# Two-layer graph network on one core: the neighbour mean split in f16 and turned by a DMA transpose instead of by TensorE

## The reference

```python
# layer 0
mask = (adj > 0)
agg  = mask @ x / max(sum(mask, 1), 1)            # the neighbour mean
out0 = relu(concat(x @ W_self + b_self, agg @ W_nb + b_nb) @ W_comb + b_comb)
x1   = layernorm(x + out0)
# layer 1
ws   = leaky_relu(attention(x1) @ attention(neigh).T)
ws   = softmax(where(adj > 0, ws, -9e15))
out  = layernorm(x1 + concat(x1 @ Wfx + bfx, ws @ (neigh @ Wv + bv)))
```

## Time and profile before

| what | value |
|---|---|
| time, median of 3 runs | 728.27 us (727.76 to 729.59) |
| time of the profiled execution | 729.11 us, its span 727.3 us |
| busy share of the span | PE 93%, VectorE 86%, ScalarE 79%, GpSimd 18% |
| DMA | 141.40 MB, mean 194 GB/s |
| matmul and transposing instructions on PE | 7368 |

### The profile page before, as it was taken

How to read it: one execution, slowest core, us unless ns; L and a number is a source line. 1 busy time by engine, 2 the same in 40 slices (tenths; PEclk the granted TensorE clock), 3 DMA queues, 4 the chain that set the end, 5 groups by cost and what they waited for, 6 DMA issues and landing times.

```text
span 727.3 us, 19837 instructions
## 1 busy us (share of the span) xinstructions
PE 677.6 (93%) x7368; PEld 599.3 (82%) x7368; DVE 622.4 (86%) x1537; ACT 571.3 (79%) x928; POOL 130.7 (18%) x243
## 2 busy tenths in 40 slices
PE   5779889999999999999999999999999999997775
PEld 4668767888888888988888888888888888886554
DVE  5888578999989999999999999999999999987863
ACT  2555248888888888888888888888888888889893
POOL 0010121212222211222211112222111222212101
PEclk9999999999999999999999999999999999999997
DMA  8977999999999999999999999999999999731222
GB/s 258 370 168 163 251 286 239 195 213 213 195 220 197 194 226 204 200 219 211 221 219 203 212 223 194 215 218 191 219 206 205 210 206 214 165 75 37 38 37 44
DMA packets 260312, 141.40 MB, mean 194 GB/s; under 512 B 225528, under 2 KB 243832, under 8 KB 260216
## 3 DMA queue, kind: packets, MB, share of 16 engines
q1 hardware_dynamic: 259688, 140.10, 90.3%
q10 hardware_dynamic: 528, 0.03, 0.0%
HBM read 81.37 MB, written 4.19 MB: 118 GB/s over the span
## 4 chain that ended last, share of the span: by engine, by line
PE 78%; DVE 5%; ACT 5%; issue 4%; DMA 3%; SPq 3%; POOL 1%; POOLq 0%; ACTq 0%; DVEq 0%
PE ps_v L1174 21%; PE agg_both L1129 14%; PE agg_both L1132 14%; PE ps_t L1153 10%; PE s_both L1144 7%; PE agg_both L1193 3%; PE agg_both L1196 3%; DMA neigh_sb<-neigh_sb 2%; PE s_both L1033 1%; PE ps_x L1213 1%; PE ps_x L1216 1%; ACT score L936 1%; DMA neigh_sb<-in_L_gnn_neigh_dram 1%; SPq L405 1%; PE agg_both L1184 1%
## 5 line engine op out<-in xcount | busy, mean ns | idle before, releaser
L1129 PE MATMUL agg_both<-x,mask_t 128*128 128x257 f16 x1024 | 244.0, 274 | 3.1 <-DMA mask_t<-mask 3.1
L1132 PE MATMUL agg_both<-x,mask_t 128*128 128x256 f16 x1024 | 237.9, 274 | 1.6 <-DVE x L546 1.6
L930 ACT ACTIVATE score<-s_both,sc 128x512 f32<-128x512 f32 x256 | 178.4, 697 | 63.9 <-PE s_both L1144 58.2
L707 DVE CUSTOM_DVE_ANT_0 score<-score,mask 128x512 f32<-128x512 f32 x256 | 176.0, 687 | 16.8 <-ACT score L930 14.3
L1174 PEld LDWEIGHTS ps_v<-v,late 128*128 128x128 f16 x2304 | 144.0, 97 | 41.2 <-DVE late L771 16.6
L1174 PE MATMUL ps_v<-v,late 128*128 128x129 f16 (+1 forms) x2304 | 162.7, 219 | 11.3 <-DVE late L788 5.7
L936 ACT ACTIVATE score<-score,exp_bias,sc 128x1024 f32<-128x1024 f32 x128 | 159.2, 1244 | 3.2 <-DVE exp_bias L716 3.2
L771 DVE TENSOR_TENSOR late<-ps_t,late 128x512 f16<-128x512 f32 x192 | 130.8, 681 | 33.1 <-ACT late L943 31.3
L943 ACT CAST late<-ps_t 128x512 f16<-128x512 f32 x192 | 114.4, 596 | 20.5 <-PE ps_t L1153 20.5
L1153 PE MATMUL ps_t<-ident,score 128*128 128x128 f32 x768 | 116.8, 275 | 4.0 <-ACT score L936 3.7
L1129 PEld LDWEIGHTS agg_both<-x,mask_t 128*128 128x128 fp8e4 x1024 | 100.6, 98 | 17.3 <-DMA mask_t<-mask 3.3
(11 more groups left out here) (140 smaller groups left out, 801.0 us busy)
## 6 DMA issues: line engine op xcount, KB each, us to landing
adj_sb<-in_adj_dram SPq DMA_DIRECT2D x128, 512.0 KB, 5.3
neigh_sb<-in_L_gnn_neigh_dram SPq DMA_DIRECT2D x8, 512.0 KB, 7.9
score<-in_x_dram SPq DMA_DIRECT2D x8, 512.0 KB, 8.6
x_in<-in_x_dram SPq DMA_DIRECT2D x32, 128.0 KB, 3.0
out_dram<-out_sb SPq DMA_DIRECT2D x32, 128.0 KB, 3.5
mask_t<-mask SPq DMA_TRANSPOSE x128, 4.7
neigh_sb<-neigh_sb SPq DMA_TRANSPOSE x64, 4.0
mask<-in_L_gnn_W_comb_dram SPq DMA_DIRECT2D x1, 512.0 KB, 8.0
```

Of the source, the lines that this page charges most:

```text
L707: dve.tensor_tensor_reduce(score[:, b % 2, part], score[:, b % 2, part], mask[:, b % MASK_BUFS, part], 1.0, -3.0e38, ALU.subtract, ALU.max ...
L930: act.activation(score[:, b % 2, k * GW:(k + 1) * GW], ps_s[k % 2][:, :], ACT.Prelu, alpha=SLOPE, scale=score_scale).then_inc(leaky_made, 1)
L1129: mm = pe.matmul(agg[:, 0:D + 1], mask_t8[:, c, 0, :], x16[:, c, X_HI:X_ONE + 1], start=(c == 0), stop=(c == NC - 1), skip_group_check=True)
L1132: mm = pe.matmul(agg[:, 0:D], mask_t8[:, c, 0, :], x16[:, c, X_LO:X_LO + D], start=False, stop=False, skip_group_check=True)
```

## The change

The mean is scaled and split into two f16 halves straight from `ps_agg`, before it is turned: `mean_high` (ScalarE, slot 8) and `mean_low` (VectorE, slot 9). One DMA transpose, `turn_mean` (SP, slot 10), turns both halves (128 x 512 f16) into `mean_t`. PE's two transposes, the ScalarE activation of `mean_of` and their semaphores go. `combine` and everything behind it stand one slot further on, and so do the four mask quarters; `aggregate`, `degrees` and `turn_x` keep their slots.

```diff
-MASK_SLOTS = (-7, -5, -1, 0)
+MASK_SLOTS = (-6, -4, 0, 1)
 MEAN_AT = 8
-MEAN_T_AT = 9
-MEAN_SPLIT_AT = 10
-MEAN_LOW_AT = 11
+MEAN_LOW_AT = 9
+MEAN_T_AT = 10
 X_TURN_AT = 4
-COMBINE_AT = 12
-LAYER0_AT = 13
+COMBINE_AT = 13
+LAYER0_AT = 14
...
-        mean = sb("mean", [P, D], F32)
-        mean_t = sb("mean_t", [P, 2, D], F16)
+        mean = sb("mean", [P, 2, D], F16)
+        mean_t = sb("mean_t", [P, 2 * DC, P], F16)
...
+            def turn_mean(b):
+                sp.wait_ge(mean_lo_made, b + 1)
+                at_least(sp, combined, b)
+                sp.dma_start_transpose(mean_t[:, :, :], mean[:, :, :].rearrange("p a d -> p (a d)")).then_inc(mean_t_in, 16)
...
                 if d := due(s, X_TURN_AT, 0):
                     turn_x(d[0])
+                if d := due(s, MEAN_T_AT, 0):
+                    turn_mean(d[0])
...
-            def mean_of(b):
+            def mean_high(b):
                 act.wait_ge(degree_step, 2 * (b + 1))
-                at_least(act, mean_t_done, b)
-                act.activation(mean[:, :], ps_agg[b % 2][:, 0:D], ACT.Copy, scale=row[:, 5:6]).then_inc(mean_made, 1)
-
-            def mean_high(b):
-                act.wait_ge(mean_t_done, b + 1)
-                at_least(act, combined, b)
-                act.activation(mean_t[:, 0, :], ps_agg[b % 2][:, 0:D], ACT.Copy, scale=x_scale).then_inc(mean_hi_made, 1)
+                at_least(act, mean_t_in, 16 * b)
+                act.activation(mean[:, 0, :], ps_agg[b % 2][:, 0:D], ACT.Copy, scale=row[:, 5:6]).then_inc(mean_hi_made, 1)
...
-            def mean_transpose(b):
-                pe.wait_ge(mean_made, b + 1)
-                for dc in range(DC):
-                    mm = pe.transpose(ps_agg[b % 2][:, dc * P:(dc + 1) * P], mean[:, dc * P:(dc + 1) * P], ident[:, :])
-                mm.then_inc(mean_t_done, 1)
-
             def combine(b):
                 if b == 0:
                     pe.wait_ge(m_split, DC)
                 pe.wait_ge(x_t_in[b % 2], 16 * (b // 2 + 1))
-                pe.wait_ge(mean_lo_made, b + 1)
+                pe.wait_ge(mean_t_in, 16 * (b + 1))
```

More of the change, by code:

```diff
@@ L51 @@
 RES_BUFS = 4
-MASK_SLOTS = (-7, -5, -1, 0)
+MASK_SLOTS = (-6, -4, 0, 1)
 MEAN_AT = 8
-MEAN_T_AT = 9
-MEAN_SPLIT_AT = 10
-MEAN_LOW_AT = 11
+MEAN_LOW_AT = 9
+MEAN_T_AT = 10
 X_TURN_AT = 4
-COMBINE_AT = 12
-LAYER0_AT = 13
[L63 to L74, removed]
+COMBINE_AT = 13
+LAYER0_AT = 14
+X1_AT = 16
+X1_T_AT = 17
+X1_COPY_AT = 18
+X1_LOW_AT = 19
+HIDDEN_AT = 20
+TANH_AT = 21
+XATT_AT = 22
+STACK_AT = 23
+SCORE_AT = 24
+ROW_MAX_AT = 32
+TURN_AT = 34
+WEIGH_AT = 35
 BY_DMA = 1
@@ L82 @@
 EXP_PLACE = [[quarter for _, quarter in EXPS].index(k) for k in range(4)]
[L83 to L87, removed]
+WIDE_HIGH_AT = (36,)
+WIDE_LOW_AT = (37,)
+WIDE_TURN_AT = (38,)
+WIDE_WEIGH_AT = (41,)
+LAYER1_AT = 43
 SLOTS = NG * (NB - 1) + LAYER1_AT + 1
@@ L294, in gnn_kernel @@
         pv_done = sem("pv_done")
-        mean_t_done = sem("mean_t_done")
+        mean_t_in = sem("mean_t_in")
         combined = sem("combined")
@@ L312, in gnn_kernel @@
         exp_made = sem("exp_made")
-        mean_made = sem("mean_made")
         mean_hi_made = sem("mean_hi_made")
@@ L720, in degrees @@
                 dve.wait_ge(agg_done, NQ * (b + 1))
-                at_least(dve, mean_made, b)
-                dve.tensor_scalar(row[:, 4:5], ps_agg[b % 2][:, D:D + 1], EDGE_F8, x_scale, ALU.max,
-                                  ALU.mult).then_inc(degree_step, 1)
+                at_least(dve, mean_hi_made, b)
+                dve.tensor_scalar(row[:, 4:5], ps_agg[b % 2][:, D:D + 1], EDGE_F8, None, ALU.max).then_inc(degree_step, 1)
                 dve.wait_ge(degree_step, 2 * b + 1)
@@ L728, in mean_low @@
                 dve.wait_ge(mean_hi_made, b + 1)
-                dve.scalar_tensor_tensor(out=mean_t[:, 1, :], in0=ps_agg[b % 2][:, 0:D], scalar=x_scale,
-                                         in1=mean_t[:, 0, :], op0=ALU.mult, op1=ALU.subtract).then_inc(mean_lo_made, 1)
+                dve.scalar_tensor_tensor(out=mean[:, 1, :], in0=ps_agg[b % 2][:, 0:D], scalar=row[:, 5:6],
+                                         in1=mean[:, 0, :], op0=ALU.mult, op1=ALU.subtract).then_inc(mean_lo_made, 1)
             def layer0(b):
@@ L983, in _ @@
                 first_part(s)
-                if d := due(s, MEAN_SPLIT_AT, 0):
-                    mean_high(d[0])
                 if d := due(s, X1_AT, 0):
@@ L1004, in _ @@
                 if d := due(s, MEAN_AT, 0):
-                    mean_of(d[0])
+                    mean_high(d[0])
                 if d := due(s, LAYER1_AT + 1, 0):
@@ L1195, in combine @@
                 for k, ((r, w), dc) in enumerate(product(HI_LO, range(DC))):
-                    mm = pe.matmul(ps_agg[b % 2][:, 0:D], mean_t[:, r, dc * P:(dc + 1) * P], m16[:, w, dc, 0:D],
+                    mm = pe.matmul(ps_agg[b % 2][:, 0:D], mean_t[:, r * DC + dc, :], m16[:, w, dc, 0:D],
                                    start=False, stop=(k == 3 * DC - 1))
@@ L1229, in _ @@
                     aggregate(*d)
-                if d := due(s, MEAN_T_AT, 0):
-                    mean_transpose(d[0])
                 if d := due(s, COMBINE_AT, 0):
```

## The result

The changed kernel takes 840.53 us (median of 6 runs, 837.66 to 844.74), the kernel before 729.42 us in the same session (727.76 to 730.16): a ratio of 1.154, 95% interval 1.151 to 1.156. It is slower, as forecast, but by 111 us instead of 74, and outside the range of 750 to 830.

The account below looks back on a forecast made before the run. PE was taken as the bound; steady waits +62, first blocks +12, last blocks -0.6 and the extra slot +0.7 made +74 on 729.1 us: 803, or 802 as median of runs. Range of 8 in 10: 750 to 830 us.

Parts of the forecast that it names:

- the wait and its cause: At `combine`, PE waits for the turned mean, which lands behind quarter 0's load in issue order: 2.7 us in the block shown.
- the steady wait: At `combine` in blocks 3 to 28: net cost 2.4 us a block, 26 x 2.4 = +62 us.
- low bound of 0.7 us a block: At `combine` in the steady part: the smallest net cost of a block, where 2.4 was expected and 3.9 the most.
- a microsecond in which PE waits is one lost: In the PE-bound middle stretch: each microsecond PE waits costs one microsecond, whatever the cause.
- 4 us each, +12: At `combine` in blocks 0 to 2, while the pipeline fills: 4 us of delay each, +12 (between 2 and 6 each).
- the extra slot: At the pipeline's two ends: one more slot, one of aggregation alone and one without it, costs +0.7 us.
- meet waits that are there anyway: In the first three blocks: some of the late mean's delay falls into existing waits, giving 4 us each.
- the shift costs nothing: In the steady part: the slot added between aggregation and combine costs no PE work; only the ends pay, +0.7 us.
- The end: In blocks 29 to 31, nearly without loads: a gain of 0.2 us each, -0.6 in all.
- on time: Rival at `combine`: the mean lands within 4.1 us, only PE's 0.21 us a block remain, 722 us; chance 10%.
- half relief: Rival at `combine`: the longer period empties the queue, 1.0 us net a block, +32 or 760 us; chance 15%.
- worse: Rival in `aggregate`: a fuller queue makes mask quarters late, a second wait comes, above 830 us; chance 4%.

Follow-up runs that it names:

- mean_ahead: The changed kernel, with SP issuing the mean's transpose in the same slot ahead of quarter 0's mask turn and load: 744.3 us, ratio 1.022.
- filler: The changed kernel plus 22 matmuls in `combine` whose product is overwritten, ahead of PE's wait for `mean_t`: 820.5 us, ratio 1.125.
- shift_only: The kernel before, PE's transposes kept, with combine, all behind it and the masks one slot later, the mean's stages unmoved: 739.9 us, ratio 1.015.
- no_shift_slot9: The changed kernel with the mean's transpose issued in slot 9 and combine, masks and all else back in the slots of before: 742.1 us, ratio 1.017.
- mean_slot9: The changed kernel with the mean's transpose issued one slot earlier (slot 9), ahead of quarter 3's turn: 727.2 us, ratio 0.996.
- shift_with_mean: The kernel before with combine, all behind it, the masks and the mean's four stages one slot later: 732.8 us, ratio 1.004.

## Why the prediction came out as it did

- **Right: the wait and its cause.** PE is the bound; the mean goes out behind quarter 0's load and lands behind it; PE waits for it at `combine`. mean_ahead shows that the place in the queue is the cause.
- **Right in size: the steady wait.** 2.4 us net for a block were forecast; 2.32 less 0.23 is 2.1. Over the middle this term was 6 us too high. (Its low bound of 0.7 us a block has 0.4 us for the landing behind the load, where the sum has 0.6; with 0.6 it is 0.9.)
- **Wrong: "a microsecond in which PE waits is one lost".** This step of the first part prices an idle microsecond at one. But 17 of the waits at `combine` up to block 28 were followed by some microseconds at 1.2 GHz, for 1.8 us each, and that is nearly all of the 31.8 us that the middle lost beyond its waits (1.22 in a block). It is the largest part of the 35 us by which the sum (74 against 110 of span) was short. The cause is shown: the same kernel's periods with and without a slow stretch differ by it, and it is gone in filler. No row of the kernel before's steady part could show it, since its PE never idles there; the range had no bound for it either.
- **Wrong: the ramp, "4 us each, +12".** With block 3's wait and the extra slot I had 15 us up to block 3's combine; it was 25.7. The waits of blocks 0 to 3 were 7.28 us (not 5), 7.06, 5.15 and 3.17. The delay did not "meet waits that are there anyway"; the order of work says that it fed itself:

```profile
88.19 0.48 DVE L742 SCALAR_TENSOR_TENSOR l<-agg_both,sc,z_bias 128x256 f32<-128x256 f32 x1 [9.35 <-PE agg_both L1188]
...
90.61 0.67 DVE L563 TENSOR_SCALAR mask<-adj_sb 128x1024 bf16<-128x1024 int32 x1
```

  This is VectorE's timeline of the changed kernel. VectorE stands idle for 9.35 us ahead of `layer0`, which waits for the late combine (1.05 us in the kernel before), and the next masks stand behind it in VectorE's order. So the next masks and their turns are late too, and with them the next mean. No run tests this step by itself. I had named `layer0` only as something that delays two things alike.
- **Wrong: the shift costs nothing.** At the ends it costs 3 us, not 0.7. In the steady part it costs 0.22 us with the transposes on PE (shift_only), and it is what makes their removal worth 0.23 us. The sum had this saving, but for a wrong reason: PE's busy 300 of 300 us hid a wait of the weight loads behind a running matmul, and with the mean left in its slot it would have been nothing (no_shift_slot9).
- **The end.** Behind block 29's combine 2.1 us were gained, 0.6 forecast.

Together: 10.6 (up to block 3) - 5.6 (steady waits) + 31.8 (beyond the waits, nearly all of it the clock) - 1.5 (end) = 35.3 us, the difference of the two sums. The period came out at 22.8 us (21.9 forecast), PE busy at 268.75 of 300.

Of the rivals, neither "on time" nor "half relief" holds; "worse" named a time above 830, but by a second wait in the aggregation, which isn't there.

## What to carry to other kernels

Price a wait on a PE that never idles at more than its length: here 2.3 us of wait cost 3.55 us in the mean, nothing to speak of on top where it was under 2.0 us, and 1.4 to 3.0 us more where it was longer. Shortening the wait by 0.43 us brought back under a third of that. Look at when the data are ready and when they are issued (5.8 us apart here): put the transfer ahead of the big ones in its queue (96 of 111 us here), or fill the gap (20 us). Look at the short slots of the ramp apart: a cover of three slots that is 7 us in the steady part was too short there, and a late stage holds up the next block's first stage if both stand in one engine's written order. A busy share of 100% doesn't say that removing work from the engine gains: ask what else waits in the same place, and check where the neighbours' stage stands against it.

## What was not expected of the hardware

- The clock of TensorE fell around waits of 2.04 us and more, 17 times in the middle, and not around the nine of 1.50 to 1.99 us. In the longest of these stretches it came back after nearly 6 us of full work (windows above); matmuls of 128 x 256 took 330 and 359 ns in the mean over all blocks at `combine`, against 272 and 273 ns before.
- The changed kernel with 22 more matmuls a block, needed for nothing, ran 2.4% faster (820.5 against 840.5 us).
- The added DMA transposes cost no time by their traffic in the steady part: in mean_slot9 the DMA share in 300 to 600 us is 1.06 (1.01 before), and the period is the shortest of all. In the ramp PE waits there for `mask_t` three times (5.2 us, with the early transpose ahead of mask quarters), once in shift_with_mean (2.1 us).
